# A two-layer graph network: the last section's loop cut from 13 steps of eight tiles to one, and 21 dense groups for 20

## The reference, cut to what matters

```python
deg = max(segment_sum(1, dst), 1); deg_isqrt = deg ** -0.5
h = relu(ln(x))
# layer 0: each edge takes its source's row through one of two weight matrices, by its type
msg = where(type == 0, h[src] @ Wd.T + bd, h[src] @ Wc.T + bc)
x = x + relu(segment_sum(msg, dst) + h @ Ws.T + bs)
# layer 1: each edge weighs its source's row by a gate
h = relu(ln(x))
g = tanh((h @ gw[:128])[dst] + (h @ gw[128:])[src] + gb)
yn = tanh(edge_weight * yes + (1 - edge_weight) * no)
e = (g + yn) * 0.5 * deg_isqrt[dst] * deg_isqrt[src]
out = x + segment_sum(h[src] * e, dst)
```

## Time and profile before

| | |
|---|---|
| median of 3 runs | 5392.17 us (5388.38 to 5398.95) |
| the profiled execution | 5411.43 us, span 5409.6 us |
| mean granted TensorE clock | 0.929 of full speed |
| TensorE matmul busy | 4380.4 us (81%) |
| VectorE busy | 4470.6 us (83%) |
| ScalarE busy | 3318.8 us (61%) |
| GpSimd busy | 3928.9 us (73%) |
| gathers (L590) in the main steps | 3760, 968 ns of each counted as busy |

### The profile page before, as it was taken

How to read it: one execution, slowest core, us unless ns; L and a number is a source line. 1 busy time by engine, 2 the same in 40 slices (tenths; PEclk the granted TensorE clock), 3 DMA queues, 4 the chain that set the end, 5 groups by cost and what they waited for, 6 DMA issues and landing times.

```text
span 5409.6 us, 123837 instructions
## 1 busy us (share of the span) xinstructions
PE 4380.4 (81%) x30900; PEld 3238.9 (60%) x30900; DVE 4470.6 (83%) x15813; ACT 3318.8 (61%) x11504; POOL 3928.9 (73%) x4029
## 2 busy tenths in 40 slices
PE   6588898988989899898467888888888878887864
PEld 4356666666666666665455666666666666665653
DVE  6888888878888888886467899898888988988973
ACT  5666777767777777775245566565656656665640
POOL 6777777767777677777727777777777777777774
PEclk9589999999999999999688999999999999999985
DMA  7777888778777787878555566565656665655544
GB/s 255 242 225 240 255 249 248 246 235 244 251 241 249 238 252 249 253 250 274 173 143 139 136 141 142 138 139 138 138 136 141 142 138 139 140 139 136 140 109 122
DMA packets 814769, 1028.32 MB, mean 190 GB/s; under 512 B 138839, under 2 KB 608379, under 8 KB 813563
## 3 DMA queue, kind: packets, MB, share of 16 engines
q1 hardware_dynamic: 677667, 752.38, 47.2%
q0 software_dynamic: 126976, 264.36, 20.0%
q10 hardware_dynamic: 9432, 3.66, 0.3%
HBM read 958.91 MB, written 60.97 MB: 189 GB/s over the span
## 4 chain that ended last, share of the span: by engine, by line
POOL 36%; issue 12%; PE 3%; DMA 3%; DVE 2%; SPq 0%; ACT 0%; DVEq 0%; POOLq 0%; ACTq 0%
POOL G L590 36%; PE PS L973 1%; DMA HTB<-t0s 1%; PE PS L961 1%; DMA NX<-t0s 1%; DMA HTB<-ini 1%; DMA OWF<-t0s 0%; DVE OHF L1217 0%; PE PS L924 0%; PE PS L1116 0%; DMA out<-OWF 0%; DVE ST L1206 0%; PE PS L992 0%; PE PS L933 0%; DMA OWF<-in_x 0%
## 5 line engine op out<-in xcount | busy, mean ns | idle before, releaser
L590 POOL DMA_INDIRECT G<-t,IDX x3760 | 3638.3, 968 | 1258.7 <-issue 1126.1
L730 ACT ACTIVATE OHF<-PS 128x384 bf16<-128x384 f32 x1960 | 960.6, 490 | 506.7 <-PE PS L961 476.4
L973 PE MATMUL PS<-CDST,OHF 128*128 128x256 bf16 x5880 | 975.1, 275 | 111.8 <-DVE CDST L1332 62.2
L822 ACT ACTIVATE ST<-PS,MV 128x1 f32<-128x1 f32 x1960 | 507.9, 259 | 562.8 <-DVE BB L1794 243.0
L1107 PE MATMUL PS<-HTB,NX 128*128 128x129 f32 x3920 | 821.6, 292 | 12.1 <-DVE NX L1780 11.0
L973 PEld LDWEIGHTS PS<-CDST,OHF 128*128 128x128 bf16 x5880 | 569.5, 99 | 432.5 <-ACT OHF L730 94.8
L1107 PEld LDWEIGHTS PS<-HTB,NX 128*128 128x128 f32 x3920 | 731.8, 197 | 157.9 <-issue 66.3
L841 ACT ACTIVATE OWF<-PS,ST 128x128 f32<-128x128 f32 x1960 | 700.6, 357 | 0.2
L1116 PE MATMUL PS<-CDST,OWF 128*128 128x256 f32 x1568 | 551.2, 435 | 174.7 <-ACT OWF L841 137.3
L833 ACT ACTIVATE ST<-ST,BASE 128x1 f32<-128x1 f32 x1960 | 558.6, 285 | 2.5
L1322 DVE TENSOR_SCALAR NX<-YN,PCODE 128x512 bf16<-128x512 int16 x980 | 324.4, 372 | 275.6 <-issue 145.9
(11 more groups left out here) (237 smaller groups left out, 8269.7 us busy)
## 6 DMA issues: line engine op xcount, KB each, us to landing
HTB<-t SPq DMA_DIRECT2D x980, 132.0 KB
HTB<-t0s SPq DMA_DIRECT2D x328, 384.0 KB
OWF<-t0s SPq DMA_DIRECT2D x326, 384.0 KB
NX<-t0s SPq DMA_DIRECT2D x326, 384.0 KB
YN<-rows SPq DMA_DIRECT2D x980, 64.0 KB
NX<-rows SPq DMA_DIRECT2D x980, 64.0 KB
G<-t,IDX POOLq DMA_INDIRECT x3760
t0s<-HTB SPq DMA_DIRECT2D x25, 384.0 KB, 3.5
```

Source lines behind the costliest of these rows:

```text
L590: eng.indirect_dma_start(out=G[:, k:k + width], out_offset=None, in_=table, in_offset=bass.IndirectOffsetOnAxis(ap=at, axis=0)).then_inc(s ...
L730: eng.activation(X0[:, k % KX, :, :].rearrange("p n w -> p (n w)"), PS[:, cell_bank(k), 0:384], ACT.Identity).then_inc(q_ev, 1)
L822: eng.activation(TH1[:, k % KW1:k % KW1 + 1], cell_slot(k)[:, D:D + 1], ACT.Tanh, bias=PDE[:, g % 2, b:b + 1]).then_inc(d_th, 1)
L973: ins = eng.matmul(PS[:, 4, 0:DW], X0[:, k % KX, n, :], CD0[:, k % KD, :], start=b == 0 and n == 0, stop=b == NB - 1 and n == 2)
```

## The change

```diff
-RUNS = ((20, 62),)
+RUNS = ((20, 62), (1, 56))
...
-TB = 104
+TB = 8
...
-        EWG = YN[:, HTE + 4 * GT:HTE + 5 * GT]
-        YG = YN[:, HTE + 5 * GT:HTE + 7 * GT].rearrange("p (g w) -> p g w", g=2)
-        HTE += 7 * GT
+        EWG = W2[:, D:D + GT]
+        YG = YN[:, HTE + 4 * GT:HTE + 6 * GT].rearrange("p (g w) -> p g w", g=2)
+        HTE += 6 * GT
...
-        STRIPS = [YN[:, HTE:HTE + D], OWF[:, 1792:1792 + D]]
+        STRIPS = [W2[:, 0:D], OWF[:, 1792:1792 + D]]
...
-                    eng.wait_ge(q_ot, (NG * NB + k) // QC + 1)
+                    eng.wait_ge(q_ot, -(-NG * NB // QC) + k // QC + 1)
...
-                    q0 = q // 8 * 8
+                    q0 = min(q // 8 * 8, NQ - 8)
...
-                for c in (2 * u, 2 * u + 1):
+                for c in range(2 * u, min(2 * u + 2, NG * NH)):
```

## The result

The changed kernel takes 5354.4 us (median of four runs, 5344.6 to 5362.8), the kernel before 5392.0 (four runs, 5388.4 to 5399.0): a ratio of 0.9929, 95% interval 0.9914 to 0.9945. That is 37.6 us less, where 53.5 had been forecast; the time lies in the forecast's own range (5318 to 5362).

What follows compares the result with a forecast made beforehand. Layer 0 was taken to run at its consumers' pace, layer 1 at the gathers'. Layer 0 with its section +15.1 and layer 1 -68.6 gave -53.5 us, 5339 us from the median; own range 5318 to 5362, 8-in-10 range 5308 to 5374.

Steps and rivals of the forecast that it cites:

- VectorE's need: Layer 1's main loop: rises from 9.55 to 9.80 us a step, still under the 10.09 that eight gathers take.
- the third rival: Layer 1: VectorE becomes the bound, a group costs 118.5 us, +68.1 in place of +50.4, total 5407 us; chance 0.10.
- Main gathers: Layer 1's main loop: 40 more gathers at 1.261 us each, +50.4 us, if gathers keep setting the pace.
- the end: Layer 1, last main gather to the output's transposes: twelve section steps fall away, -119.0 us.
- The eighth gather of the section: End of layer 1: might be held back wholly by VectorE's long ACC multiplication, up to 6.8 us worse, or not at all.
- The section of layer 0: Layer 0's section loop, first matmuls to layer 1's transposes: one step instead of 13 removes 93.9 us.
- the stretch ahead of it: Between layer 0's main loop's end and the section's first matmuls: work on ACC that the change leaves alone.
- Layer 0's main loop: Consumers set the pace; one more group ends the loop 109 us later (105.7 to 113.4, outer bounds 95 to 125).
- the second rival: Layer 0: joints and denser steps cost extra, loop ends 125 to 145 us later, total 5355 to 5374; chance 0.10.
- the credit of up to 7.7 us: Layer 0's main loop: the new group adds five steps where the mean group holds 10.85, saving 0 to 7.7 us.
- The 19 us of the profiled execution: Profiled execution lay 19 us above the 5392.2 median, stage unknown; the forecast change was taken off the median.
- The first rival: Gathers set the pace of both layers; layer 0 with its section -43, total -112, 5280 us; chance 0.14, whole or halfway.

Runs made afterwards that it cites:

- e1: Kernel before with the section loop's last wait (for VectorE's part of ACC) written inside the loop instead of behind it; 5398.8 us, ratio to before 1.0011.
- e4: Changed kernel with the section kept at 13 steps (21 groups, 228 main steps), so the added group alone; 5452.0 us, ratio to before 1.0110.
- e2: Changed kernel with the section loop's last wait written inside the loop instead of behind it; 5356.6 us, ratio to before 0.9940.
- e3: Changed kernel without the 21st group (20 groups, 247 main steps, one section step), so the shortened section alone; 5364.7 us, ratio to before 0.9947.
- e8: Changed kernel with layer 0's degree-count reduction replaced by a copy of a quarter of its input; 8068 us on the second chip (before there: 8071).

## Why the prediction held, and where it was off

**What bounds each layer.** Right. Layer 1 went by the gathers: 1.259 to 1.261 us apart in the six profiles of the first comparisons and of e1 to e4, with 228, 235, 240 and 247 steps. VectorE's need was forecast at 9.80 us a step; it is ((5272.11 - 2854.21) - 81.2) / 240 = 9.74. Its need in e4 was 10.0 a step at 9.03 cells, with 8.5 us of cover left, so the third rival stood close to its edge and still did not come. Taking VectorE, 91.5% busy, for the bound would have led to the third rival's 5407 us, slower than before.

**Layer 1's terms.** Right. Main gathers +50.4 forecast, +48.2 and +50.5 measured; the end -119.0, measured -119.9 twice. The eighth gather of the section, feared for 6.8 us, starts at 5282.11, 0.87 us before the multiplication (5282.98), and takes its usual 0.94, so it is not held. That was close: those of before and e1, 0.41 and 0.35 us ahead, were held. But no cost of being held shows: the section's first matmuls start 22.7 us behind the last main gather in before and e1, with the eighth gather held, 21.9 in after and e2 and 22.8 in e3, without.

**The section of layer 0.** Right: -93.9 forecast, -93.6 and -94.8 measured, and the stretch ahead of it, taken for unchanged, is 4.1 and 1.7 us shorter.

**Layer 0's main loop.** This is the term that was mis-sized: +109 forecast (105.7 to 113.4, outer bounds 95 to 125). The first pair of traces gives +102.9, but its "before" is the long execution. The second pair gives +125.7. By the medians it is -37.6 less layer 1's -72.3 and the section's -93.6, with the -4.1 ahead of it, +132; by e1's and e2's, -42.2 + 73.0 + 94.8 + 1.7, +127. Both lie outside the forecast's outer bounds for this term. So the size is that of the second rival (125 to 145). What the forecast said of who paces whom was right: GpSimd's waits rose to 151.5 where about 160 was expected, and the additions are (2711.48 - 442.87) / 20 = 113.4 us apart.

Where the missing 20 us are is inferred, not shown. The mean distance over all additions is (2608.61 - 443.19) / 19 = 114.0 and (2584.6 - 444.6) / 19 = 112.6 in the two traces of before, 113.4 and 113.3 in those of after: taken as they are, the four show no longer groups. If each execution's offset from its median (+19, -10, -10, -14) is laid on layer 0's loop, where the two traces of before differ, these become 113.0, 113.2, 113.9 and 114.0. Then the group costs 114, not 109, and the other 19 cost 0.8 to 0.9 more each, 16 in sum: 130. In e4 the same working gives 114.1, with still fewer steps a group (10.0, for 10.9 before and 10.6 after). So the credit of up to 7.7 us for steps that the new group lacks is not borne out, and neither is the second rival's reason, that ten-step groups are dearer: e4 has no others, and its groups come to the same 114. Inside one trace the steps do show. In both traces of after a ten-step span took 112.8 and 113.5 us on the mean and an eleven-step one 116.7 (8 and 10 spans, the last two left out); the prediction had read no such difference from two ten-step spans. The possibility of longer spans stood in the outer bound alone (nine ten-step spans for three, 1.5 us each: 122), with the chance of the second rival, 0.10, which was too little. The total stayed in its range with some luck: the section with the stretch ahead of it gave 3 to 4 us more than forecast, and so did layer 1.

**The 19 us of the profiled execution.** Taking them off the total fits what was measured. Not knowing their stage cost nothing in the sum, but it misleads whoever subtracts only the first two traces: -66.8 us with layer 0 at +5.2, where the medians say -37.6 with layer 0 at +35.

**The first rival** (gathers set both layers' pace, 5280 us) was wrong with 21 groups. With 20 groups on the same shortened section it is what happens in layer 0 (e3): with the added dense group GpSimd waits again (152 us), though the time is hardly another. **The range** (5308 to 5374) held.

What stays open: what sets the 114 us of a group in layer 0 (TensorE, VectorE or the ring of table parts), whether and why all groups became 0.8 us longer, and what makes the two slow chips slow.

## What to carry to other kernels

Where a ring joins a producer with a fixed pace to consumers with another, write down both needs per layer and take the larger; a step moved into the main loop is free only while the consumers are the slower side, and beyond that it costs the producer's full price (here the shortened section brings -34 us alone, the added group +53 alone, both -42, and the 8 us between -34 and -42 are within the noise). When a forecast starts from one profiled execution, find out in which stage executions scatter before its offset from the median is spread over the sum: here 24 us lay in one loop, and the stage paced by gathers repeated to 1 us. And run the kernel before beside every experiment: the same program took 5393 us on one chip and 8277 on another.

## What the runs showed of the hardware

- One program, three chips: 5393, 8071 and 8277 us, each repeating within 1%. On the slow ones GpSimd waits for TensorE for some 2900 of 8070 us (e8), and with half of layer 0's gathers that layer alone returns to 117 us a group.
- A gather is held for as long as a long VectorE instruction on ACC lasts: 7.29 us beside 6.82, 13.60 beside 13.42. Beside the one-input form it ends 0.12 us behind VectorE where it started up to 0.41 us ahead or together with it, and 0.81 to 0.82 behind where it started 0.13 us later or more; beside the two-input form, started 0.64 and 1.03 us later, it ends 0.82 behind. Gathers that started 0.62 to 0.89 us ahead of the one-input form, or 0.21 and 0.61 ahead of the two-input one, took their usual 0.94.
- Where GpSimd waits for nobody, the start-to-start distance of the gathers is 1.288 us in layer 0 and 1.259 in layer 1, both in e3; the mean gather takes 0.98 us there and 0.96 here.
